# Quantised feed-forward: the rounding constant is subtracted on Pool, three groups of "up" stay on chip, the gate is rounded in place

## The reference, cut to what matters

```python
def act_qdq(x):
    qmax = 2.0 ** (ACT_BITS - 1) - 1.0            # ACT_BITS = 16
    scale = jnp.maximum(jnp.max(jnp.abs(x)) / qmax, 1e-12)
    return jnp.clip(jnp.round(x / scale), -qmax - 1.0, qmax) * scale
...
x = act_qdq(x)
up = act_qdq(x @ lpbq_dequant(w_up).T)            # 256 -> 768
gate = act_qdq(x @ lpbq_dequant(w_gate).T)
sig = fixed_qdq_u16(jax.nn.sigmoid(gate))         # rounded to 1/65536
gate = act_qdq(gate * sig)
o = act_qdq(gate * up)
return o @ lpbq_dequant(w_down).T                 # then added to x and normalised
```

## Time and profile before

| | us |
|---|---|
| median of 3 runs (2762.44 to 2764.74) | 2763.64 |
| the profiled execution, its own time | 2754.06 |
| its span, from first to last instruction | 2752.3 |
| projection block, first DVE instruction to last maximum | 2370.6 to 2511.2 |
| gating block, first ACT instruction to last group's maximum | 2514.7 to 2580.9 |
| product block, first ACT instruction to last group's maximum | 2583.6 to 2643.6 |
| last block, to the end | 2646.1 to 2752.3 |
| a store of "up" in the projection block, issue to landing (median) | 4.3 |

### The profile page before, as it was taken

The page is one execution under the profiler, slowest core; times in us unless marked ns, Lnnn a source line. Parts: engine busy times, 40 slices in busy tenths (PEclk is TensorE's granted clock), DMA queues, the critical chain, the costliest instruction groups (busy, mean ns, idle before and its releaser), DMA issues. The chain is left out here.

```text
span 2752.3 us, 53362 instructions
## 1 busy us (share of the span) xinstructions
PE 2338.3 (85%) x18240; PEld 1861.4 (68%) x18240; DVE 1546.6 (56%) x2929; ACT 1221.1 (44%) x2701; POOL 609.3 (22%) x682
## 2 busy tenths in 40 slices
PE   8989999778999999389957999999999996694047
PEld 5669999677999999277754666666666665452035
DVE  5866666583111111379963666666666665645865
ACT  2223333212434343156643565555555564436733
POOL 1101111155444444154431111121111210000000
PEclk9999999968999999689977999999999998797579
DMA  2223222183999999400006555455554552110211
GB/s 80 64 61 78 74 65 65 23 271 109 343 342 347 343 344 340 134 7 0 0 25 139 126 126 128 118 128 127 125 128 118 126 126 63 49 72 36 107 42 42
DMA packets 386450, 346.73 MB, mean 126 GB/s; under 512 B 70322, under 2 KB 364748, under 8 KB 384332
## 3 DMA queue, kind: packets, MB, share of 16 engines
q1 hardware_dynamic: 321612, 302.19, 36.7%
q10 hardware_dynamic: 52480, 26.83, 3.9%
q0 software_dynamic: 12288, 16.79, 2.8%
HBM read 258.72 MB, written 87.05 MB: 126 GB/s over the span
## 5 line engine op out<-in xcount | busy, mean ns | idle before, releaser
L2087 ACT COPY rel_probT<-rel_ps_t 121x400 f32<-121x400 f32 x384 | 196.8, 512 | 251.9 <-PE rel_ps_t L2319 251.9
L2099 ACT ACTIVATE rel_prob<-rel_ps_s,rel_nmx 100x361 f32<-100x361 f32 x512 | 264.9, 581 | 1.4 <-DVE rel_nmx L2201 1.4
L2319 PE MATMUL rel_ps_t<-rel_ident,rel_prob 100*121 100x100 f32 x1536 | 242.0, 280 | 7.3 <-ACT rel_probT L2087 7.3
L2319 PEld LDWEIGHTS rel_ps_t<-rel_ident,rel_prob 100*121 100x121 f32 x1536 | 195.6, 185 | 77.4 <-ACT rel_probT L2087 48.9
L1266 PEld LDWEIGHTS moe_ps_h<-moe_xeT,moe_w 128*128 128x128 f32 x2048 | 240.2, 193 | 5.1 <-issue 1.9
L1266 PE MATMUL moe_ps_h<-moe_xeT,moe_w 128*128 128x128 f32 x2048 | 240.7, 276 | 1.3 <-DVE moe_xeT L1431 1.3
L2201 DVE TENSOR_REDUCE rel_nmx<-rel_ps_s 100x2 f32<-100x722 f32 x256 | 232.8, 909 | 8.8
L1266 PE MATMUL moe_ps_y<-moe_w,moe_hT 128*128 128x256 f32 x1024 | 231.5, 379 | 0.0
L2832 PE MATMUL ffd_ps_y<-ffn_w_dT,ffd_oq 128*100 128x256 f32 x384 | 86.1, 386 | 145.7 <-DVE ffd_oq L2777 140.1
L1266 PEld LDWEIGHTS moe_ps_y<-moe_w,moe_hT 128*128 128x128 f32 x1024 | 189.6, 190 | 23.2
L1257 ACT ACTIVATE moe_hT<-moe_ps_h,moe_b 128x128 f32<-128x128 f32 x512 | 142.9, 376 | 137.4 <-PE moe_ps_h L1266 137.1
(11 more groups left out here) (427 smaller groups left out, 4958.7 us busy)
## 6 DMA issues: line engine op xcount, KB each, us to landing
moe_w<-in_L_ffn_w SPq DMA_DIRECT2D x128, 1024.0 KB, 9.6
rel_scores<-rel_r_ext SPq DMA_DIRECT2D x32, 818.8 KB
rel_r_key<-rel_scores SPq DMA_DIRECT2D x32, 818.8 KB
rel_weights<-rel_prob ACTq DMA_DIRECT2D x128, 204.7 KB
rel_by_dist<-rel_weights SPq DMA_DIRECT2D x32, 400.0 KB
mut_ctx_nat<-in_ctx SPq DMA_DIRECT2D x32, 363.0 KB
mut_ctx_T<-in_ctxT SPq DMA_DIRECT2D x16, 722.0 KB
rel_ctx_T<-in_ctxT SPq DMA_DIRECT2D x32, 361.0 KB, 3.4
```

Source lines behind the costliest of these rows:

```text
L2087: nc.scalar.copy(probT[:, pg % 2, c], ps_pT).then_inc(s_t_sb, 1)
L2099: last = nc.scalar.activation(prob[:, t.parity, slot, :], ps_s[0:S, j, 0:L], ACT.Exp, bias=nmx[:, slot:slot + 1])
L2319: last = nc.tensor.transpose(ps_pT[:, j, :], prob[:, pt.parity, QUAD * pg + j, c * STEP:c * STEP + R], ident[0:S, 0:S])
```

## The change

In the gating block ACT no longer subtracts ROUND; Pool does, in place in `gate`, and the tile `whole` is gone. ACT rounds two groups ahead. In the product block DVE no longer subtracts ROUND from "up"; Pool does. ACT now rounds "up" first and then the gate, the gate in place instead of in `gr`. DVE takes the maximum of the group before after the product, not ahead of it. The tile for "up" becomes `up_kept`, three buffers that live through the whole stage: the last three groups (5, 6, 7) are not stored, stay there, and come first in the product block; the other five are stored and loaded as before. In the projection block the loops are written out.

```diff
@@ quantised_ffn
+        up = o.sb("up_kept", [P, 3, IC, N])
+        KEPT = range(GROUPS - 3, GROUPS)
@@ projection block (ffp); every engine's turns(...) becomes groups(turn, -1)
-            up = m.sb("up", [P, 2, IC, N])
+            def groups(turn, first):
+                for i in range(first, GROUPS):
+                    turn(Turn(i, i % 2, i // 2))
...
-                                act.wait_ge(s_up[t.parity], 16 * t.half)
+                            if n == 0 and t.i > 2:
+                                act.wait_ge(s_up[t.i % 3], 16 * (t.i // 3))
...
+                for t in range(GROUPS):
+                    if t not in KEPT:
+                        sp.wait_ge(s_h_sb, NH * t + IC)
+                        sp.dma_start(up_rows[t], up[:, t % 3]).then_inc(s_up[t % 3], 16)
@@ gating block (ffs), scalar
                 def rounded(g):
-                    if g > 2:
-                        act.wait_ge(s_g, g - 2)
-                    nc.scalar.activation(whole[:, g % 3], gate[:, g], ACT.Identity, bias=consts[:, 0:1], scale=g_inv).then_inc(s_r, 1)
+                    nc.scalar.activation(gate[:, g], gate[:, g], ACT.Identity, bias=round_c[:], scale=g_inv).then_inc(s_r, 1)
 
                 rounded(0)
+                rounded(1)
                 for g in range(GROUPS):
-                    act.wait_ge(s_r, g + 1)
-                    nc.scalar.activation(whole[:, g % 3], whole[:, g % 3], ACT.Identity, bias=consts[:, 1:2]).then_inc(s_n, 1)
-                    if g + 1 < GROUPS:
-                        rounded(g + 1)
                     act.wait_ge(s_n, g + 1)
                     if g > 2:
                         act.wait_ge(s_g, g - 2)
-                    nc.scalar.activation(sig[:, g % 3], whole[:, g % 3], ACT.Sigmoid, scale=g_scale).then_inc(s_s, 1)
+                    nc.scalar.activation(sig[:, g % 3], gate[:, g], ACT.Sigmoid, scale=g_scale).then_inc(s_s, 1)
+                    if g + 2 < GROUPS:
+                        rounded(g + 2)
+
+            @block.gpsimd
+            def _(pool):
+                for g in range(GROUPS):
+                    pool.wait_ge(s_r, g + 1)
+                    nc.gpsimd.tensor_scalar(gate[:, g], gate[:, g], ROUND, None, ALU.subtract).then_inc(s_n, 1)
@@ gating block, vector: in1 of L2670 becomes gate[:, g]
@@ product block (ffo)
-            up = m.sb("up", [P, 3, IC, N])
-            gr = m.sb("gr", [P, 3, IC, N])
+            ORDER = list(KEPT) + [g for g in range(GROUPS) if g not in KEPT]
+            HOME = [g % 3 for g in KEPT]
...
+                for n in range(len(KEPT), GROUPS):
+                    sp.wait_ge(s_o, n - 2)
+                    sp.dma_start(up[:, HOME[n % 3]], up_rows[ORDER[n]]).then_inc(s_up[n], 16)
...
+                for n, g in enumerate(ORDER):
+                    mine = up[:, HOME[n % 3]]
+                    if n >= len(KEPT):
+                        act.wait_ge(s_up[n], 16)
+                    nc.scalar.activation(mine, mine, ACT.Identity, bias=round_c[:], scale=u_inv).then_inc(s_ur, 1)
+                    nc.scalar.activation(gate[:, g], gate[:, g], ACT.Identity, bias=round_c[:], scale=a_inv).then_inc(s_gr, 1)
+
+            @block.gpsimd
+            def _(pool):
+                for n in range(GROUPS):
+                    mine = up[:, HOME[n % 3]]
+                    pool.wait_ge(s_ur, n + 1)
+                    nc.gpsimd.tensor_scalar(mine, mine, ROUND, None, ALU.subtract).then_inc(s_uq, 1)
...
-                    dve.wait_ge(s_ur, g + 1)
-                    nc.vector.tensor_scalar(up[:, g % 3], up[:, g % 3], ROUND, None, ALU.subtract).then_inc(s_uq, 1)
...
+                for n, g in enumerate(ORDER):
+                    dve.wait_ge(s_gr, n + 1)
+                    dve.wait_ge(s_uq, n + 1)
+                    nc.vector.scalar_tensor_tensor(out=gate[:, g], in0=gate[:, g], scalar=ROUND, in1=up[:, HOME[n % 3]],
                                                    op0=ALU.subtract, op1=ALU.mult).then_inc(s_o, 1)
+                    if n:
+                        largest(n - 1)
```

More of the change, by code:

```diff
@@ L2549, in turn @@
                                                     apply_absolute_value=True).then_inc(s_top, 1)
-                turns(dve, turn, -1, 1, GROUPS - 1, GROUPS)
+                groups(turn, -1)
             @block.scalar
@@ L2568, in turn @@
                             act.wait_ge(s_h, NH * t.i + (n + 1))
-                            if n == 0 and (not isinstance(t.i, int) or t.i > 1):
-                                act.wait_ge(s_up[t.parity], 16 * t.half)
-                            out = up[:, t.parity, c, :] if k == 0 else gate[:, bass.ds(t.i, 1), c, :].rearrange("p a n -> p (a n)")
+                            if n == 0 and t.i > 2:
+                                act.wait_ge(s_up[t.i % 3], 16 * (t.i // 3))
+                            out = up[:, t.i % 3, c, :] if k == 0 else gate[:, bass.ds(t.i, 1), c, :].rearrange("p a n -> p (a n)")
                             nc.scalar.copy(out, ps_h[:, n % 4, 0:N]).then_inc(s_h_sb, 1)
-                turns(act, turn, -1, 1, GROUPS - 1, GROUPS)
+                groups(turn, -1)
             @block.sync
             def _(sp):
[L2578 to L2584, removed]
+                for t in range(GROUPS):
+                    if t not in KEPT:
+                        sp.wait_ge(s_h_sb, NH * t + IC)
+                        sp.dma_start(up_rows[t], up[:, t % 3]).then_inc(s_up[t % 3], 16)
+                for v in range(3):
+                    sp.wait_ge(s_up[v], 16 * len([t for t in range(GROUPS) if t not in KEPT and t % 3 == v]))
             @block.tensor
@@ L2669, in _ @@
                     dve.wait_ge(s_sr, g + 1)
-                    nc.vector.scalar_tensor_tensor(out=gate[:, g], in0=sig[:, g % 3], scalar=ROUND_16, in1=whole[:, g % 3],
+                    nc.vector.scalar_tensor_tensor(out=gate[:, g], in0=sig[:, g % 3], scalar=ROUND_16, in1=gate[:, g],
                                                    op0=ALU.subtract, op1=ALU.mult).then_inc(s_g, 1)
@@ L2697, in _ @@
                 act.wait_ge(s_const, 2)
-                for g in range(GROUPS):
-                    if g > 2:
-                        act.wait_ge(s_o, g - 2)
-                    nc.scalar.activation(gr[:, g % 3], gate[:, g], ACT.Identity, bias=round_c[:], scale=a_inv).then_inc(s_gr, 1)
-                    act.wait_ge(s_up[g], 16)
-                    nc.scalar.activation(up[:, g % 3], up[:, g % 3], ACT.Identity, bias=round_c[:], scale=u_inv).then_inc(s_ur, 1)
+                for n, g in enumerate(ORDER):
[10 more added lines that the diff above has]
+                    nc.gpsimd.tensor_scalar(mine, mine, ROUND, None, ALU.subtract).then_inc(s_uq, 1)
             @block.vector
```

27 lines of the change are left out of this document (8 added, 19 removed).

## The result

The changed kernel takes 2821.28 us (median of 4 runs, 2816.44 to 2823.65) against 2764.19 for the kernel before: ratio 1.0204, 95% interval 1.0189 to 1.0219, so 52 to 61 us slower. The forecast was 2756.1, range 2746 to 2772. It was wrong in sign and in size.

What follows compares the result with a forecast made beforehand. PE bounds the projection block, ACT gating with DVE 0.2 us behind, DVE the product block. Gating +1.0 and product -8.5 give -7.5 us: 2763.6 to 2756.1 us, range 2746 to 2772.

Steps and rivals of the forecast that it cites:

- The price of Pool's operation: Gating and product blocks: Pool's subtraction of a constant on 128 x 2400 takes 2.4 us, ends 2.1 and 7.0.
- Rival 2: Both blocks: Pool's operation is slow; at 4.6 to 5.1 us the kernel is 28 us slower, 2791; chance 0.20.
- The exclusion: Both blocks: DVE's one-input and two-input operations and Pool's hold each other; a held DVE operation costs Pool's remainder less 0.2 us.
- rival 3: Both blocks: DVE's two-input operation does not stop for Pool, only Pool for it; 17 us faster, 2746.6; chance 0.17.
- That the reduction excludes nothing: Both blocks: DVE's reduction does not exclude Pool, so Pool's 2.4 us fits beneath its 2.57; otherwise the gain is gone.
- The walk through gating: Gating block: Pool's pushes on DVE sum to 6.8 us against 5.8 saved, so it ends 1 us later.
- the pushes by late loads: Product block: Pool, its input late from a load, pushes a product; 2.4 us twice or 2.3 once; 8.5 saved taken.
- if nothing collides: Product block: with no collision between Pool and DVE it ends at 2631.8 against 2643.6, 11.8 us saved.
- Costed at nothing: Rest of the change, gate rounded in place, fewer stores and written-out loops in the projection block: no effect on time.

Runs made afterwards that it cites:

- The run of prices: Kernel before, with 17 Pool operations on scratch tiles added in the projection block; subtraction 6.3 to 6.6 us, add then mult 2.2 to 2.5.
- the fast form: Changed kernel with Pool's subtraction written as add -ROUND, then times 1.0, in both blocks; 2759.4 us against 2761.4, ratio 0.9999.

## Why the prediction was wrong, step by step

**The price of Pool's operation is the step that failed.** I took 2.4 us, between 2.1 and 7.0; alone it is 6.3 to 6.6. The row that had it right was the tensor-scalar with 100 elements in 536 ns, the only one of the same instruction at a size that tells anything (it multiplies, but also with one operator alone). I set it aside as a fixed cost of fetching a scalar, and went by the select and the copy, other operations. The run of prices shows a scalar from memory at 6.35 us, no different from a constant, so that reading was wrong: 2.8 ns an element, as the row said, against 2.5 to 2.8 measured. The two-input row scaled to 4.6, and so it is for its own form (4.51, L2641), but that form is cheaper than the subtraction of a constant. With 2.2 us in its place (the fast form) the kernel came to 2759.4, no change from before. By the blocks it gained 1.8 us (+4.1, -5.9) of the 7.5 forecast, so the right price alone would not have made the forecast true; the rest is below.

**Rival 2 was the case that came, and its price was too small.** It gave a break-even at T of 3.0 and 28 us of loss at T of 4.6 to 5.1. At 6.4 the loss is 57 us. Its two parts were +19 and +9, measured +34.4 and +19.6.

**The exclusion was right, both ways.** DVE stands until Pool is done, in the one-input and in the two-input operation, so rival 3 falls: a product of 5.54 beside L2714. The earlier trace rows had shown this for the one-input operation alone; for the two-input one they show that Pool stops for it, and that it stops for Pool as well was an assumption, which came true. That the reduction excludes nothing, which I had assumed, holds: 2.63 to 2.65 in every run. When DVE lets go and Pool waits, Pool is next: in the gating block of the changed kernel the held rows fit a Pool operation after every DVE operation that holds the port, as long as Pool has one ready.

**The walk through gating was right for the T it assumed.** Pushes of 1.6, 2.1, 2.1 and 1.0 us were worked out, 1.5, 2.0, 2.0 and 1.0 measured in the fast form. The block came out 4.1 us longer than before, not 1.0, as the first DVE operation started 11.4 us after ACT's first, where I had 8.3.

**A term was missing: the late first start.** It was put at nothing: Pool's first subtraction was to start when ACT's first rounding ended, and starts 4.3 to 4.6 us after it in each block, 6.1 to 7.4 when nothing overlaps. No row of before shows it for a tensor-scalar, since Pool has none after a reduction over partitions there.

**In the product block the pushes by late loads came once in three traces.** I took one or two pushes of 2.2 us. With the fast form in both blocks the first two products were held, by Pool's late start and not by a load; from the third on DVE's products kept 2.64 us, and Pool waited for them instead and worked beneath the next reduction. With Pool in the product block alone one push by a load did come (4.58 us at 2632.04). Without the late start the block took 48.1 us, 11.9 under before, against 11.8 "if nothing collides" and the 8.5 I took; that it had no push hangs on a tenth of a microsecond: in two traces Pool's row starts 0.01 to 0.02 us ahead of the product's (2622.52 and 2622.53; 2630.53 and 2630.55) and Pool waits, in the third 0.11 ahead and DVE waits.

**Costed at nothing, and so measured:** written-out loops, fewer stores, in-place rounding (no Pool at all: gating 66.2; projection 133.3 us from first to last maximum, 133.2 before). Keeping three groups and rounding "up" first took 4.8 us off the product block with DVE's old work.

What stays open: why a subtraction with one operator runs 2.5 to 3 times slower than add, then mult; only the operators above were tried. An addition of -ROUND with one operator alone was not run, so whether it is the subtraction or the single operator that is slow is not shown. The row of the multiplication (2.8 ns an element) points to the single operator; add, then subtract (8.33) shows that a second one by itself doesn't help.

## What to carry to other kernels

Price a Pool operation by a row of the same instruction with the same operators and as many of them, at a size where the slope shows, and if there is none, measure it first: the same arithmetic cost 6.3 or 2.2 us by its spelling. Work that goes to Pool beside DVE takes the port from DVE's one-input operations on SBUF, and, if Pool reads, from its two-input ones; of the DVE operations tried here only the reduction is cover, and a DVE instruction can stand for the whole of Pool's. Before moving a small operation between engines, ask if another engine's output conversion makes it unnecessary: that was worth 17 us of the 18.5 here.

## What the runs showed of the hardware that I had not expected

- Pool's tensor-scalar on 128 x 2400 float32: 6.3 to 6.6 us with subtract alone, 4.51 as a two-input operation with one column, 8.33 with add and subtract, 2.2 to 2.5 with add and mult or mult and add.
- Changing between the reduction over partitions and a tensor-scalar on Pool costs 6.1 to 7.4 us, in either direction and within a block; a memset in between starts on time. It shows as "issue" behind a pair of MODIFY_POOL_CONFIG on Pool's sequencer, and where Pool would have waited anyway part of it is hidden.
- Conversion to 16-bit integers on ACT's output (2.29 us) and reading them on DVE (2.65 us) cost no more than float32 does for tiles of 128 x 2400 (2.38 and 2.65).
